# The delta branch's output normalisation moved behind the next tile's projections and convolutions

## The reference, cut to what matters

```python
h = _rms(x, attn_norm_w)
q = silu(silu(_causal_dwconv(h @ Wq.T, conv_q)))      # k and v in the same way
q = _l2norm(q); k = _l2norm(k)
beta = sigmoid(h @ Wbeta.T)
o, memory_state = _delta_scan(k, q, v, beta)          # sequential over the tokens
o = _rms(o, out_norm_w) @ Wout.T
x = x + o                                             # called y below
h2 = _rms(x, mlp_norm_w)
x = x + silu(h2 @ Wgate.T) * (h2 @ Wup.T) @ Wdown.T
```

## Time and profile before

| | |
|---|---|
| median of 3 runs | 1544.53 us (1538.68 to 1551.4) |
| the profiled execution | 1549.48 us, its span 1547.7 us |
| mean granted TensorE clock | 0.819 of full speed |
| PE busy | 1138.0 us, 74% |
| DVE busy | 969.1 us, 63% |
| ACT busy | 477.7 us, 31% |
| POOL busy | 172.7 us, 11% |

### The profile page before, as it was taken

One profiled execution on the slowest core, in us unless ns is written; L12 is line 12 of the kernel. 1 busy time (PEld: TensorE's weight loads), 2 busy tenths in 40 slices (PEclk: granted clock), 3 DMA queues, 4 the chain that ended last, 5 costly groups with the idle time before them and its releaser, 6 DMA issues.

```text
span 1547.7 us, 22181 instructions
## 1 busy us (share of the span) xinstructions
PE 1138.0 (74%) x8568; PEld 752.1 (49%) x8568; DVE 969.1 (63%) x2520; ACT 477.7 (31%) x995; POOL 172.7 (11%) x251
## 2 busy tenths in 40 slices
PE   5378547878877777878877887878887887777037
PEld 3146414555546544665445553655445554565025
DVE  3421376866777576865677575865777576846941
ACT  1024402434323412443332422433333422342011
POOL 2000000400031000400030010400030000400300
PEclk8579757979879887899878887989878887999559
DMA  9430413042211413041211414051301403001000
GB/s 294 40 33 5 55 62 33 2 61 67 31 18 36 50 56 33 2 70 56 35 14 40 54 47 33 1 69 58 40 9 41 64 30 33 1 14 61 0 14 7
DMA packets 112426, 64.76 MB, mean 42 GB/s; under 512 B 49184, under 2 KB 106688, under 8 KB 112320
## 3 DMA queue, kind: packets, MB, share of 16 engines
q1 hardware_dynamic: 109264, 58.19, 22.2%
q10 hardware_dynamic: 3056, 5.15, 1.2%
HBM read 45.73 MB, written 17.17 MB: 41 GB/s over the span
## 4 chain that ended last, share of the span: by engine, by line
PE 45%; DVE 25%; DMA 9%; SPq 7%; ACT 7%; issue 7%; POOL 1%; DVEq 0%; POOLq 0%; ACTq 0%
PE bank L1415 8%; PE bank L1395 5%; PE bank L1400 4%; DMA k_stack<-k_pieces 4%; PE bank L1334 4%; DVE k_l L1112 3%; PE bank L1553 3%; PE bank L1504 3%; DVE lane_buf L327 3%; PE bank L1326 2%; PE bank L1372 2%; PE bank L1576 2%; DVE lane_buf L1082 2%; DMA q_stack<-m_rows 2%; DVE conv L973 2%
## 5 line engine op out<-in xcount | busy, mean ns | idle before, releaser
L649 ACT ACTIVATE probs<-bank 128x512 f32<-128x512 f32 x256 | 149.2, 599 | 164.5 <-PE bank L1400 164.2
L903 DVE TENSOR_REDUCE mx<-bank 128x2 f32<-128x320 f32 x256 | 123.4, 491 | 84.1 <-PE bank L1372 75.2
L1415 PE MATMUL bank<-probs,v_ext 128*16 128x128 f32 x2048 | 160.8, 283 | 15.7 <-ACT probs L649 14.7
L1367 PE MATMUL bank<-edge_mask,identb 128*128 128x64 bf16 x512 | 70.0, 227 | 100.8 <-DMA k_stack<-k_pieces 43.3
L327 POOL TENSOR_TENSOR lane_buf<-state,q_l 128x128 f32<-128x128 f32 x128 | 87.8, 715 | 486.6 <-DVEq L1107 486.6
L1395 PE MATMUL bank<-tri_mask,identb 128*128 128x512 bf16 x256 | 112.8, 441 | 30.2 <-DMA q_stack<-m_rows 30.2
L1082 DVE TENSOR_TENSOR lane_buf<-state,til 128x128 f32<-128x128 f32 x256 | 104.1, 407 | 19.4 <-POOL lane_buf L537 10.1
L1367 PEld LDWEIGHTS bank<-edge_mask,identb 128*128 128x128 bf16 x512 | 35.2, 109 | 160.3 <-DVE mx L903 71.4
L1400 PE MATMUL bank<-q_stack,k_stack 128*128 128x128 bf16 x1024 | 112.4, 239 | 0.0
L1415 PEld LDWEIGHTS bank<-probs,v_ext 128*16 128x16 f32 x2048 | 87.0, 98 | 49.5 <-ACT probs L649 26.1
L1400 PEld LDWEIGHTS bank<-q_stack,k_stack 128*128 128x128 bf16 x1024 | 89.3, 108 | 39.7 <-issue 16.3
(11 more groups left out here) (156 smaller groups left out, 1918.7 us busy)
## 6 DMA issues: line engine op xcount, KB each, us to landing
k_stack<-k_pieces SPq DMA_DIRECT2D x192, 64.0 KB
q_stack<-q_pieces SPq DMA_DIRECT2D x192, 32.0 KB
q_l<-lane_q SPq DMA_DIRECT2D x8, 512.0 KB, 4.0
k_l<-lane_k SPq DMA_DIRECT2D x8, 512.0 KB, 4.7
q_pieces<-conv SPq DMA_DIRECT2D x24, 128.0 KB, 2.1
k_pieces<-conv SPq DMA_DIRECT2D x48, 64.0 KB, 2.0
x<-in_x SPq DMA_DIRECT2D x8, 256.0 KB, 2.8
x_in<-in_x SPq DMA_DIRECT2D x8, 256.0 KB, 8.5
```

The lines of the kernel that those rows point to most:

```text
L649: act.activation(probs[:, u % 3], score_bank[u % 3][:], ACT.Exp, scale=float(DK) ** -0.5).then_inc(exp_done, 1)
L903: dve.tensor_reduce(mx[:, g, 2 * v:2 * v + 2], bank[1 + u % 2][:, 0:2 * SPAN].rearrange("p (h k) -> p h k", h=2), AX.X, ALU.max).then_inc( ...
L1367: pe.matmul(edges[:, :, e * W:e * W + SUB], identb[:], edge_mask[:, e * SUB:(e + 1) * SUB].rearrange("p (o s) -> p o s", o=1) .broadcast_t ...
L1415: last = pe.matmul(bank[5][row:row + VE, col:col + W], v_ext[:, b, kb, h, :], probs[:, u % 3, (hp * 2 + kb) * W:(hp * 2 + kb + 1) * W], st ...
```

## The change

Only the order in the bodies changes; no instruction is added, removed or resized.

- PE: `output_sums` and `output_product` go from ahead of `turn_a(n, 3)`, `beta_in` and `delta_in` to behind them.
- ACT: `output_squares` goes from ahead of `norms_z` to between `raw_of(n, 1)` and `raw_of(n, 2)`; `output_rstd` and `y_norm` go behind `raw_of(n, 2)`.
- DVE: `output_norm` goes from ahead of `z_of` to behind `convolve(n, 1)`; `y_of` and `y_tok` go behind `convolve(n, 2)` and `keep_taps`, and `act_of(t, 0)` with them.

```diff
@@ ACT body
-                if scan:
-                    output_squares(t)
-                    output_rstd(t)
                 if following:
                     norms_z(n)
                     turn_a(n, 3)
                     beta_exp_of(n)
+                    for s in range(2):
+                        raw_of(n, s)
                 if scan:
+                    output_squares(t)
+                if following:
+                    raw_of(n, 2)
+                if scan:
+                    output_rstd(t)
                     y_norm(t)
-                if following:
-                    for s in range(3):
-                        raw_of(n, s)
                 if scan:
                     turn_c(t, 1)
@@ DVE body
                 if following:
                     second_residual(n, has_scan)
-                if has_scan:
-                    output_norm(t)
                 if following:
                     z_of(n)
-                if has_scan:
-                    y_of(t)
-                if following:
                     z_tok(n)
                     beta_of(n)
-                if has_scan:
-                    y_tok(t)
-                if following:
                     convolve(n, 0, front)
                     convolve(n, 1, front)
                 if has_scan:
-                    act_of(t, 0)
+                    output_norm(t)
                 if following:
                     convolve(n, 2, front)
                     keep_taps()
+                if has_scan:
+                    y_of(t)
+                    y_tok(t)
+                    act_of(t, 0)
                 if has_scan:
                     act_of(t, 1)
                     act_of(t, 2)
@@ PE body
+                if following:
+                    turn_a(n, 3)
+                    beta_in(n)
+                    delta_in(n)
                 if scan:
                     output_sums(t, front)
                     output_product(t)
-                if following:
-                    turn_a(n, 3)
-                    beta_in(n)
-                    delta_in(n)
                 if scan:
                     turn_c(t, 1)
                     for i in range(IT):
```

More of the change, by code:

```diff
@@ L1201, in body @@
                     second_residual(n, has_scan)
+                if following:
+                    z_of(n)
+                    z_tok(n)
+                    beta_of(n)
+                    convolve(n, 0, front)
+                    convolve(n, 1, front)
                 if has_scan:
@@ L1204, in body @@
                 if following:
-                    z_of(n)
+                    convolve(n, 2, front)
+                    keep_taps()
                 if has_scan:
                     y_of(t)
-                if following:
-                    z_tok(n)
-                    beta_of(n)
-                if has_scan:
                     y_tok(t)
-                if following:
-                    convolve(n, 0, front)
-                    convolve(n, 1, front)
-                if has_scan:
                     act_of(t, 0)
-                if following:
-                    convolve(n, 2, front)
-                    keep_taps()
                 if has_scan:
@@ L1591, in body @@
                     ffn_down(n)
-                if scan:
-                    output_sums(t, front)
-                    output_product(t)
                 if following:
@@ L1598, in body @@
                     delta_in(n)
+                if scan:
+                    output_sums(t, front)
+                    output_product(t)
                 if scan:
```

## The result

The changed kernel takes 1591.38 us (median of 4 runs, 1587.39 to 1599.98) against 1546.88 us for the kernel before (4 runs): the two medians lie 44.5 us apart. The recorded ratio is an estimate of its own and not the quotient of these medians (which is 1.0288): 1.0313, interval 1.0279 to 1.0347, so +43 to +54 us. The profiled execution is one of 1587.39 us with a span of 1585.6 us, 37.9 us longer than that of before.

A forecast was written before the change was run, and what follows sets the result against it. No engine alone bounds it; the order of engines' waits does. Losing 76 us behind the first convolution and gaining 35 ahead gives +41: profiled 1549.5 becomes 1590.5, forecast 1585 since that execution lies 5 above the median; range 1566 to 1601.

The forecast's parts named there:

- A after: Residual (L946) to first convolution (L971): 13.0 us a body, 12.6 to 13.4; 35 us gained over seven bodies.
- B after: First convolution to square_sums (L1514): 28.1 us a body against 17.2 before; 76 us lost over seven bodies.
- upper end: First convolution to square_sums with PE at half clock from the product on, as in body t = 7: 28.5 us.
- lower end: First convolution to square_sums with PE at full clock, product hidden behind the third convolution: 26.8 us.
- The mechanism, gate_up behind the convolutions: PE's gate_up, which ran beside the convolutions, waits for y_of behind them: 10.9 us a body.
- y_tok beside POOL's residual: DVE's y_tok could be blocked on the shared port, adding 1.0 us a body; t = 7's trace says not.
- Rows 7 as a template for gate_up: Body t = 7, output_norm to gate_up's end with nothing beside it: 21.92 us; the silus would fit beside it.
- The clock holds: Rival: PE's idle stretches too short to drop the clock at turn_c and gate_up; +29, 1574 us; chance 0.18.
- More is lost: Rival: every body at the half-clock bound, z's chain slow, y_tok blocked by POOL; +53, 1598 us; chance 0.13.
- It does less: Rival: read-back or ffn's end sets z, so residual to first convolution hardly falls; 76 us or 1620; chance 0.04.
- Faster: Rival: convolutions and second silu end the stage, first convolution to square_sums stays 17.2 us; -35, 1509 us; chance 0.05.

The follow-up runs named there:

- second execution: The changed kernel once more, unaltered, for a second profiled execution and more times: 1595.2 us, ratio 1.0278.
- PE kept busy: Changed kernel with 15 never-read matmuls behind output_sums and 20 behind output_product in seven bodies: 1570.15 us, ratio 1.0149.
- y late alone: Kernel before with only y_of, y_tok, act_of(0) behind the three convolutions and y_norm behind the third raw copy: 1602.88 us, ratio 1.0356.
- one convolution earlier: Changed kernel with output_norm behind the first convolution and y_of and y_tok behind the second: 1564.82 us, ratio 1.0123.
- silus first: Changed kernel with the first two silu_twice on ScalarE ahead of y_norm: 1614.14 us, ratio 1.0439.
- woven with PE kept busy: Kernel before with the outputs' norm woven into gaps of z's chain, plus 14 never-read matmuls ahead of output_sums: 1517.26 us, ratio 0.9805.

## Why the prediction was right

The forecast was 1585 us in a range of 1566 to 1601, and 1591.4 was measured. Step by step:

- A after, 13.0 us a body (12.6 to 13.4). Measured: 12.62 to 13.55, mean 13.01. The body without a back half was the right model, PE's clock included; the two bodies at 13.55 lie just over the upper bound, and one at 12.36 in the second execution just under the lower. The gain was 35.4 us.
- B after, 28.1 us (26.8 to 28.5). Measured: 27.72 to 28.73, mean 28.07, so 76.3 us lost. The two ends turned out to be mixed. In two bodies (28.71 and 28.73) the product ran at half clock throughout (3.78 us) and y_of came 11.2 us behind the first convolution, as in the upper end, which was short by 0.2. In the other five the product took 2.5 to 2.8 us and was done behind the third convolution, so that y_of came at 10.6, as in the lower end, and only turn and gate_up had the half clock of the upper (27.72 to 27.87). The forecast did not work out this mix. 28.1 was chosen between 26.8 and 28.5, and that the mean came within 0.03 of it is luck; the second execution has 27.92. The lower end was 26.8, and PE kept busy reached 26.61: the clock's share of B, put at 1.3 us above a full clock, is 1.46. With that kernel the clock term is shown by an experiment.
- The mechanism, gate_up behind the convolutions. Shown from both sides: y late alone gives 73.0 of B's 76.3 us without moving sums or product, and y one convolution earlier takes some of it back. That silus queued behind y_norm were to blame is excluded by silus first.
- y_tok beside POOL's residual. The trace agrees with the row of t = 7: y_tok takes 0.62 us and is not blocked; the residual ends ahead of it.
- Rows 7 as a template for gate_up. It takes 12.4 to 12.8 us with the silus beside it (12.52 at t = 2), and 12.52 at t = 7 of before without them.
- The time. Of the 6.4 us between 1585 and 1591.4, 2.4 are the base: before was taken at 1544.5, and its median is now 1546.9. What the sum of +40.9 leaves open is the distance to +44.5. The two profiled executions of each kernel give +40.9 and +39.9 in the stage; the intervals of the ratio (+43 to +54 us, and +29 to +57 when timed again) hold or nearly touch it, and outside the stage executions of one kernel differ by 4 to 9 us. Nothing more was shown.
- The rivals. "The clock holds" was made to happen by the kernel with PE kept busy, where A and B give +28.1 us against the +29 said. "More is lost" came true only in part: two bodies were at the upper end of B, and y_tok was blocked in none. "It does less" is out, since A fell to 13. "Faster" would have needed B under 22.2; the smallest B of any kernel with y behind a convolution was 26.5.
- Two slips in the numbers, neither of which decides anything. "It does less" ends at 1620 us, so its 0.04 belongs to "slower by over 1%", which makes 0.95 and leaves nothing for "within 1%". And 1574 less the 6 us of spread is 1568, not 1566, while the upper bound of 1601 is not worked out from a term (1598 and 6 would be 1604).

What I did not see is how A could be had at no price. Nearly two thirds of its gain comes from the one exchange of z_tok and y_of, which leaves y where it was. That version, 1523.4 us, beats both kernels and is the simplest of those that do; woven with PE kept busy has the lowest median, 1517.3, but its interval overlaps.

## What to carry to other kernels

When two chains share engines, moving one of them out of the other's way pays only for the stretch in which it really was in the way, and its own follow-up work (here 48 matmuls of gate_up) moves with it: look at what runs beside the stage now and ask where it will run. Start with the smallest exchange that removes the wait, since the chain of waits names it: z_tok stood behind an instruction whose result it does not use. A body of the same loop that lacks one of the halves was a good model of the reordered body here (A 13.0 forecast, 13.01 measured), since it holds the clock's state too. Matmuls added to hold the clock have to fit into time in which PE would wait anyway: put ahead of work that is ready, they delay it.

## What the runs showed of the hardware that was not expected

- Matmuls whose result nobody reads shortened the time: 35 in a body brought the changed kernel from 1591.4 to 1570.2 us, of which 12.9 us are traced to the stage. Through gate_up the granted clock stayed at 1.00 (2.4 GHz) where it had been at 0.50 (1.2 GHz), and gate_up's f32 matmuls followed it. The Trainium skill, "TensorE: Matmul & The Clock Gate", Part 1, has activity release the throttle, and these runs agree; that it pays on a whole kernel is shown here.
- The gain is fragile: in the woven kernel with PE busy, one gap of 1.42 us and one of 0.68 us, behind 14 added matmuls and four sums, were followed at t = 2 by a product at half clock for most of its length (3.66 us in place of 1.99). This was so in part or whole in five bodies; in the other two the product, begun equally late behind the residual (6.89 us), took 1.99. What decides between them was not found.
- A norm with Ln and Exp behind a Silu cost two table loads of 1.28 us, one ahead of each function, where the kernel asks for the set that holds both only once a body. In the changed kernel that norm stands ahead of the silus and costs none.
